# A selective state-space loop with its three elementwise steps dealt out anew: input product on the vector engine from PSUM, decay in PSUM, output product on GpSimd

## The chip, the cores and the metric

The kernel runs on one core of a Trainium2 chip. The metric is the device time in microseconds (us) of one execution. The kernel before was timed three times: 2757.33, 2756.4 and 2756.42 us, so the median is 2756.42 us.

A core has five engines with instruction queues of their own: TensorE (PE, matrix products), VectorE (DVE), ScalarE (ACT), GpSimd (POOL) and SyncE (SP, which here only starts DMAs). Each runs its own program in order. They are tied together by semaphores: an instruction adds to a semaphore when it has finished, and `wait_ge(s, n)` holds the queue of an engine until the semaphore `s` has reached `n`. SBUF is the on-chip memory of 128 partitions; PSUM is the smaller one that TensorE writes, here 8 banks of 128x512 f32 numbers.

## The reference, cut to what matters

The input is x of shape (4, 1024, 128), that is 4 batches of 1024 positions and 128 features. A layer has a state-space part (`_L0_attn_ref`) and an attention part with a mixture of 32 experts (`_L0_ffn_ref`). The change is in the state-space part alone, in these lines:

```python
Bm = h @ w_B.T + b_B                      # (batch, 1024, 16)
Cm = h @ w_C.T + b_C                      # (batch, 1024, 16)
Delta = softplus((h @ w_d1.T + b_d1) @ w_d2.T + b_d2)
A_bar = exp(-Delta[..., None] * A)        # decay, one for each of the 16 states
BX = (Delta * h)[..., None] * Bm[:, :, None, :]
# states[t] = A_bar[t] * states[t-1] + BX[t], along the 1024 positions
_, states = associative_scan(comb, (A_bar, BX), axis=1)
y = einsum('blfn,bln->blf', states, Cm) + D * h
```

For each batch and for each of 16 states four 128x1024 arrays are made (features on the partitions, positions along the row): the decay, the driving term bx = (Delta h) B, the state by a running scan, and the product cs = state x C. The 16 products are summed to y.

## The kernel before, in words

The batches are done one after the other (`Fori(0, BATCH)` on every engine). Each has a state-space stage, then eight head pairs of attention, then the experts. The stages are closed by `part_end`, which all five engines must reach. The order within a stage is written out by hand: each engine has its own instruction list, and only semaphores order one against another.

The state loop runs over n = 0 to 15. It uses PSUM bank pairs 2-3 (the row of B spread over all partitions), 4-5 (the row of C spread likewise) and 6-7 (the sum y). The steps of one state are:

- PE `broadcast_b` (line 1271): two bf16 products that write the B row of state n into banks 2-3. PE `broadcast_c` (line 1279): the same for C in banks 4-5.
- ACT line 712: copies banks 2-3 into `b_rows` in SBUF. ACT line 717: the decay, exp of `delta` times a column, into `decay` in SBUF.
- POOL line 538: bx = `du` x `b_rows`, all in SBUF.
- DVE line 964: the scan, `state` from `decay` and `bx`. DVE line 970: cs = `state` x banks 4-5.
- PE `add_state` (line 1286): adds cs into banks 6-7 by a product with the identity, two calls of 512 columns in f32; the trace has them as four matmul records.

`decay`, `b_rows`, `bx`, `state` and `cs` have two buffers each, which alternate with n. Semaphores for free buffers start above zero (`CREDITS`, line 365). So `cs_ready`, which starts at 2, reaches i + 3 when the product cs of state i is made, and `add_state(i)` waits for exactly that.

PE's list before is broadcast_b(0), b(1), c(0), and then for m = 0 to 13: broadcast_b(m+2), broadcast_c(m+1), add_state(m); at the end c(15), add(14), add(15). DVE's list is scan(n), product(n), for each n. After the loop DVE line 972 multiplies banks 6-7 with the gate, and what follows it is the output norm and projection of the stage. Before the loop DVE line 957 makes `du`; its signal is `delta_ready`.

Of the kernel before, what the change touches and what calls it, by code (L numbers as in the profile page):

```python
# [7 lines left out]
ALU = mybir.AluOpType  # L8
ACT = mybir.ActivationFunctionType
AX_X = mybir.AxisListType.X  # L10
F32 = mybir.dt.float32
# [3 lines left out]
P = 128  # L15
BATCH, SEQ, DM = 4, 1024, 128
# [4 lines left out]
STATES = 16  # L21
# [138 lines left out]
def program(nc, ins, out):  # L160
    with ExitStack() as ctx:
        def sb(name, shape, dt=F32, where=None):
            return (where or ctx).enter_context(nc.sbuf_tensor(name, shape, dt))

        def sem(name):
            return ctx.enter_context(nc.semaphore(name))
# [9 lines left out]
        neg_a = sb("neg_a", [P, STATES])  # L176
# [48 lines left out]
        m_ctx = ExitStack()  # L225
# [12 lines left out]
        sp_log = sb("sp_log", [P, SEQ], F32, m_ctx)  # L238
        delta = sb("delta", [P, SEQ], F32, m_ctx)
        du = sb("du", [P, SEQ], F32, m_ctx)  # L240
        decay = sb("decay", [P, 2, SEQ], F32, m_ctx)
        b_rows = sb("b_rows", [P, 2, SEQ], F32, m_ctx)
        bx = sb("bx", [P, 2, SEQ], F32, m_ctx)
        state = sb("state", [P, 2, SEQ], F32, m_ctx)
        cs = sb("cs", [P, 2, SEQ], F32, m_ctx)
# [66 lines left out]
        def banks(a, n=2):  # L312
            return ps[:, a:a + n, :].rearrange("p a n -> p (a n)")
# [5 lines left out]
        passed, part_done, weights_in = sem("passed"), sem("part_done"), sem("weights_in")  # L319
# [10 lines left out]
        a_out, a_taken = sem("a_out"), sem("a_taken")  # L330
        v_out, v_taken = sem("v_out"), sem("v_taken")
        tok_ready, v_norm, yg_ready = sem("tok_ready"), sem("v_norm"), sem("yg_ready")

        bc_out, bc_ready, delta_ready = sem("bc_out"), sem("bc_ready"), sem("delta_ready")
        b_bcast, b_taken, c_bcast = sem("b_bcast"), sem("b_taken"), sem("c_bcast")
        decay_ready, bx_ready, scanned, cs_ready, cs_used = (
            sem("decay_ready"), sem("bx_ready"), sem("scanned"), sem("cs_ready"), sem("cs_used"))

# [3 lines left out]
        proj_out, proj_taken = sem("proj_out"), sem("proj_taken")  # L342
# [16 lines left out]
        moe_taken, y_stored = sem("moe_taken"), sem("y_stored")  # L359
# [2 lines left out]


        DOWN_FREE = HALVES * SLOTS
        CREDITS = [(proj_out, 2 * 10), (y_stored, 16), (a_taken, 2), (v_taken, 2), (scanned, 2), (bx_ready, 2),
                   (cs_used, 2), (b_taken, 1), (cs_ready, 2),
                   (proj_taken, PROJ_BANKS), (scores_taken, 3), (blocks_taken, 2), (pv_out, NU), (v_added, ADDS), (p_added, ADDS),
                   (ctx_ready, 4),
                   (high_a, 1), (high_p, 1), (low_ready, 1), (roped_ready, 1), (inverted, 1), (misc_taken, 1),
# [21 lines left out]
        PARTS, V_ANGLES, V_FIRST, V_STEPS, V_OUTS, A_OUTS, A_STEPS = 3, 14, 23, 118, 6, 20, 7  # L391
# [20 lines left out]
        def root_at(b, k):  # L412
            return 2 + b * RSTDS + k + 1
# [75 lines left out]
        def _(pool):  # L489
            for s, c in CREDITS:  # L490
                pool.sem_inc(s, c)
# [18 lines left out]
            def inverse_root(at, n, eps=EPS):  # L510

                pool.wait_ge(ms_ready, at)
                pool.sem_inc(passed, 1)
                pool.tensor_scalar(ms[:, 0:n], ms[:, 0:n], eps, None, ALU.add).then_inc(ms_plus, 1)
                pool.wait_ge(ms_plus, at)
                pool.tensor_tensor(rstd[:, 0:n], ms[:, 0:n], neg_half[:, 0:n], ALU.pow).then_inc(rstd_ready, 1)
# [3 lines left out]
            with pool.Fori(0, BATCH) as b:  # L520
# [6 lines left out]
                                              b_out_r.unsqueeze(1).broadcast_to((P, TILES, P)), ALU.add))  # L527
                inverse_root(root_at(b, R_CONV), 1)

                pool.wait_ge(delta_ready, b + 1)  # L530
                pool.sem_inc(passed, 1)
                with pool.Fori(0, STATES // 2) as r:
                    for k in range(2):
                        n = b * STATES + 2 * r + k
                        pool.wait_ge(b_taken, n + 2)

                        pool.wait_ge(scanned, n + 1)
                        pool.tensor_tensor(bx[:, k, :], du[:, :], b_rows[:, k, :], ALU.mult).then_inc(bx_ready, 1)  # L538
                inverse_root(root_at(b, R_GATED), TILES)
                part_end(pool, PARTS * b + 2)  # L540

# [20 lines left out]
                def step(s, par, this, prev, prev2):  # L562
# [4 lines left out]
                    for k in range(2 if this else 0):  # L567
# [9 lines left out]
                        for i in (2 * k, 2 * k + 1):  # L577
                            pool.sem_inc(passed, 1)
                            pool_copy(pool, *copies[i]).then_inc(high_p, 1)
                            pool.wait_ge(high_p, 4 * n + i + 2)  # L580
                            pool.sem_inc(passed, 1)
                    for kind, _, u in slots(prev, this):
                        if kind == "low":

# [67 lines left out]
        def _(act):  # L652
# [20 lines left out]
            with act.Fori(0, BATCH) as b:  # L673
                def take(k, n, dst, func, bias=0.0, scale=1.0):

                    act.wait_ge(a_out, b * A_OUTS + k + 1)
                    act.activation(dst, ps[0:n, k % 2, :], func, bias=bias, scale=scale).then_inc(a_taken, 1)
# [25 lines left out]
                act.preload_act_table(ACT.Exp)  # L703
                for c in range(2):
                    take(10 + c, 96, bc3[:, c * HALF:(c + 1) * HALF], ACT.Identity)
                with act.Fori(0, STATES // 2) as r:
                    for k in range(2):
                        n = b * STATES + 2 * r + k
                        act.wait_ge(b_bcast, n + 1)

                        act.wait_ge(bx_ready, n + 1)
                        act.activation(b_rows[:, k, :], banks(2), ACT.Copy).then_inc(b_taken, 1)  # L712
                        act.wait_ge(delta_ready, b + 1)

                        act.wait_ge(scanned, n + 1)
                        act.sem_inc(passed, 1)
                        act.activation(decay[:, k, :], delta[:, :], ACT.Exp,
                                       scale=neg_a[:, bass.ds(2 * r + k, 1)]).then_inc(decay_ready, 1)
                for c in range(2):
                    take(12 + c, P, gT[:, c * HALF:(c + 1) * HALF], ACT.Identity)  # L720
                part_end(act, PARTS * b + 2)
# [111 lines left out]
        def _(dve):  # L833
# [93 lines left out]
            with dve.Fori(0, BATCH) as b:  # L927
# [27 lines left out]
                dve.wait_ge(a_step, A_STEPS * b + 6)  # L955
                st.link(dve.scalar_tensor_tensor(delta[:, :], z[:, :], 0.0, sp_log[:, :], ALU.max, ALU.add))
                dve.tensor_tensor(du[:, :], delta[:, :], h_act[:, :], ALU.mult).then_inc(delta_ready, 1)
                with dve.Fori(0, STATES // 2) as r:
                    for k in range(2):
                        n = b * STATES + 2 * r + k  # L960
                        dve.wait_ge(decay_ready, n + 1)
                        dve.wait_ge(bx_ready, n + 3)
                        dve.wait_ge(cs_ready, n + 1)
                        dve.tensor_tensor_scan(state[:, k, :], decay[:, k, :], bx[:, k, :], 0.0, ALU.mult, ALU.add  # L964
                                               ).then_inc(scanned, 1)
                        dve.wait_ge(scanned, n + 3)
                        dve.wait_ge(c_bcast, n + 1)

                        dve.wait_ge(cs_used, n + 1)
                        dve.tensor_tensor(cs[:, k, :], state[:, k, :], banks(4), ALU.mult).then_inc(cs_ready, 1)  # L970
                dve.wait_ge(cs_used, STATES * b + STATES + 2)
                dve.tensor_tensor(hc[:, :], banks(6), gate[:, :], ALU.mult).then_inc(yg_ready, 1)

# [223 lines left out]
        def _(pe):  # L1197
# [13 lines left out]
            def cut(t, c, shift=0):  # L1211
                return t[:, c * HALF + shift:(c + 1) * HALF + shift]
# [19 lines left out]
            with pe.Fori(0, BATCH) as b:  # L1232
# [33 lines left out]

                def broadcast_b(i):

                    pe.wait_ge(b_taken, b * STATES + i + 1)
                    for c in range(2):  # L1270
                        made = pe.matmul(ps[:, 2 + c, :], fold[:, bass.ds(i, 1)].broadcast_to((96, P)),
                                         cut(bc3, c), start=True, stop=True)
                    made.then_inc(b_bcast, 1)

                def broadcast_c(i):

                    pe.wait_ge(cs_ready, b * STATES + i + 2)
                    for c in range(2):
                        made = pe.matmul(ps[:, 4 + c, :], fold[:, bass.ds(STATES + i, 1)].broadcast_to((96, P)),
                                         cut(bc3, c), start=True, stop=True)  # L1280
                    made.then_inc(c_bcast, 1)

                def add_state(i, k):
                    pe.wait_ge(cs_ready, b * STATES + i + 3)
                    for c in range(2):
                        made = pe.matmul(ps[:, 6 + c, :], ident[:, :], cut(cs[:, k, :], c), start=False, stop=False,  # L1286
                                         skip_group_check=True)
                    made.then_inc(cs_used, 1)

                broadcast_b(0)  # L1290
                broadcast_b(1)
                broadcast_c(0)
                with pe.Fori(0, STATES // 2 - 1) as r:
                    for k in range(2):
                        broadcast_b(2 * r + k + 2)
                        broadcast_c(2 * r + k + 1)
                        add_state(2 * r + k, k)
                broadcast_c(STATES - 1)
                add_state(STATES - 2, 0)
                add_state(STATES - 1, 1)  # L1300
# [305 lines left out]
```

## Time and profile before

| What | Value |
|---|---|
| Median of three runs | 2756.42 us |
| Span of the profiled execution | 2757.4 us |
| PE busy (share of the span) | 2292.2 us (83%) |
| DVE busy | 2103.8 us (76%) |
| POOL busy | 1243.0 us (45%) |
| ACT busy | 1162.1 us (42%) |
| Scans, line 964, 64 of them | 207.4 us |
| bx on POOL, line 538, 64 | 171.4 us |

The profile is of one execution whose own time is its span, 2757.4 us, with nothing told beside it; that is 1.0 us above the median. Busy shares are means over stages with quite different limits. The profile also gives the TensorE clock that was granted in a stretch, as a share of the full 2.4 GHz: 1.00 is 2.4 GHz, 0.50 is 1.2 GHz, and a figure between them is a mean over a stretch with both. "Idle before, releaser" tells how long an engine stood idle ahead of an instruction and which other instruction ended that.

### The profile page before, as it was taken

What the parts mean: (1) busy time and instruction counts of PE and PEld (TensorE: products, weight loads), DVE (VectorE), ACT (ScalarE), POOL (GpSimd) and SP (SyncE); (2) the same over time, 40 slices, a digit from 0 to 9 for tenths busy, and PEclk for the clock granted to TensorE, in tenths of its full rate; (3) what the DMA queues carried; (4) which work ended last, traced back from release to release, by engine and by line L of the source; (5) the groups of instructions that cost most, each with busy time, mean ns of one, the idle gap of its engine ahead of it and who ended that gap; (6) DMA issues with size and microseconds to landing.
All of it is one profiled execution on the core that took longest, in us unless ns stands there. A gap on an engine that the chain in (4) does not pass through costs nothing.

```text
span 2757.4 us, 45423 instructions
## 1 busy us (share of the span) xinstructions
PE 2292.2 (83%) x11606; PEld 1361.5 (49%) x11606; DVE 2103.8 (76%) x3267; ACT 1162.1 (42%) x1889; POOL 1243.0 (45%) x1058
## 2 busy tenths in 40 slices
PE   3649999879665999997966599999796669999889
PEld 1235555547323555554732455564572245555456
DVE  4868888769496888876948688886794878888678
ACT  3413443337541434344743143443474223434256
POOL 2544555433253646443325465554333455556332
PEclk9779999989886999998978799999897879999889
DMA  1000000001000000000100000000100000000011
GB/s 56 0 23 5 5 8 4 0 19 41 11 0 23 5 9 4 4 0 25 36 9 0 23 5 9 4 4 1 31 30 9 0 23 5 8 8 0 3 34 33
DMA packets 36374, 35.84 MB, mean 13 GB/s; under 512 B 4008, under 2 KB 31120, under 8 KB 36240
## 3 DMA queue, kind: packets, MB, share of 16 engines
q1 hardware_dynamic: 36240, 34.27, 4.2%
q8 instruction: 58, 0.95, 0.1%
q14 instruction: 76, 0.62, 0.1%
HBM read 32.16 MB, written 2.10 MB: 12 GB/s over the span
## 4 chain that ended last, share of the span: by engine, by line
PE 58%; DVE 18%; issue 10%; ACT 7%; POOL 5%; DVEq 1%; ACTq 0%; DMA 0%; POOLq 0%; SPq 0%
PE ps L1431 8%; PE ps L1446 7%; PE ps L1216 6%; PE ps L1217 5%; PE ps L1218 5%; PE ps L1413 4%; DVE state L964 4%; PE ps L1415 3%; PE ps L1332 3%; PE ps L1286 3%; POOL bx L538 3%; PE ps L1491 2%; ACT q_split L750 2%; PE ps L1244 2%; DVE inverse L1007 2%
## 5 line engine op out<-in xcount | busy, mean ns | idle before, releaser
L767 ACT ACTIVATE probs<-ps 128x512 f32<-128x512 f32 (+3 forms) x768 | 356.5, 488 | 510.8 <-PE ps L1418 282.0
L1071 DVE TENSOR_REDUCE tops<-ps 128x1 f32<-128x512 f32 (+3 forms) x768 | 387.7, 545 | 116.7 <-PE ps L1446 81.7
L612 POOL TENSOR_TENSOR prob_sums<-prob_sums,probs 128x512 f32<-128x512 f32 (+3 forms) x256 | 237.8, 929 | 334.4 <-ACT probs L767 322.5
L1446 PE MATMUL ps<-k_high,q_split 128*128 128x512 f32 (+3 forms) x768 | 323.0, 435 | 41.9 <-POOL k_high L484 35.0
L1413 PE MATMUL ps<-q_split,k_high 128*128 128x512 f32 (+3 forms) x768 | 324.5, 423 | 21.8 <-ACT probs L767 15.5
L1431 PE MATMUL ps<-probs,vals 128*64 128x512 f32 (+3 forms) x1536 | 325.4, 509 | 0.0
L1415 PE MATMUL ps<-q_max,k_low 65*128 65x512 f32 (+7 forms) x768 | 268.9, 350 | 0.0
L1446 PEld LDWEIGHTS ps<-k_high,q_split 128*128 128x128 f32 x768 | 159.1, 208 | 218.0 <-issue 112.0
L574 POOL TENSOR_TENSOR roped<-turned 128x1024 f32<-128x1024 f32 x64 | 155.4, 2429 | 239.2 <-DVE turned L1048 226.3
L538 POOL TENSOR_TENSOR bx<-du,b_rows 128x1024 f32<-128x1024 f32 x64 | 171.4, 2691 | 199.9 <-ACT b_rows L712 163.8
L964 DVE TENSOR_TENSOR_SCAN state<-decay,bx 128x1024 f32<-128x1024 f32 x64 | 207.4, 3240 | 42.9 <-POOL bx L538 42.9
L742 ACT ACTIVATE q_max<-ps 1x512 fp32r<-1x512 f32 x128 | 75.2, 588 | 377.1 <-PE ps L1332 376.3
L1174 DVE TENSOR_TENSOR hg_low<-hg,hg_high 128x512 fp32r<-128x512 f32 x256 | 231.3, 903 | 0.7 <-ACT hg_high L805 0.7
L797 ACT ACTIVATE hid<-ps,cols 128x512 f32<-128x512 f32 x256 | 176.5, 689 | 101.9 <-PE ps L1218 73.8
L1413 PEld LDWEIGHTS ps<-q_split,k_high 128*128 128x128 f32 x768 | 151.3, 197 | 121.2 <-ACT probs L767 84.3
L1169 DVE TENSOR_TENSOR hg<-hid,ps 128x512 f32<-128x512 f32 x256 | 174.6, 682 | 46.9 <-ACT hid L797 35.2
L484 POOL TENSOR_SCALAR w_high<-w 128x256 fp32r<-128x256 f32 x128 | 56.6, 442 | 282.9 <-PE ps L1218 280.4
L1098 DVE TENSOR_TENSOR prob_sums<-prob_sums,probs 128x512 f32<-128x512 f32 (+3 forms) x256 | 181.1, 707 | 0.4
L805 ACT ACTIVATE hg_high<-hg 128x512 fp32r<-128x512 f32 x256 | 159.4, 623 | 1.9 <-PE ps L1218 1.4
L1286 PE MATMUL ps<-cs,ident 128*128 128x512 f32 x256 | 152.4, 730 | 0.0
L1216 PE MATMUL ps<-hg_high,w_high 128*128 128x512 f32 x256 | 149.5, 584 | 2.6 <-DVE hg_low L1174 2.6
L1415 PEld LDWEIGHTS ps<-q_max,k_low 65*128 65x128 f32 (+1 forms) x768 | 149.0, 194 | 4.1
(230 smaller groups left out, 4937.6 us busy)
## 6 DMA issues: line engine op xcount, KB each, us to landing
w<-in_w SPq DMA_DIRECT2D x128, 128.0 KB, 2.1
w_pair<-in_w_pairs SPq DMA_DIRECT2D x36, 256.0 KB, 2.6
xin<-in_x SPq DMA_DIRECT2D x5, 512.0 KB, 3.8
out<-acc SPq DMA_DIRECT2D x4, 512.0 KB, 4.1
pos<-in_c_pos SPq DMA_DIRECT2D x1, 512.0 KB, 4.8
v_w<-in_v_w SPq DMA_DIRECT2D x1, 512.0 KB
o_w<-in_o_w SPq DMA_DIRECT2D x1, 512.0 KB
v_b<-in_v_b SPq DMA_DIRECT2D x1, 512.0 KB
```

Of the source, the lines that this page charges most:

```text
L538: pool.tensor_tensor(bx[:, k, :], du[:, :], b_rows[:, k, :], ALU.mult).then_inc(bx_ready, 1)
L612: pool.tensor_tensor(total, before, probs[:, u % RING, 1, at:HALF], ALU.add).then_inc(p_added, 1)
L767: act.activation(probs[:, u % RING, h, q0 - HALF * c:HALF], ps[:, 4 + h, 0:w], ACT.Exp, scale=SCALE).then_inc(blocks_taken, 1)
L964: dve.tensor_tensor_scan(state[:, k, :], decay[:, k, :], bx[:, k, :], 0.0, ALU.mult, ALU.add).then_inc(scanned, 1)
L1071: dve.tensor_reduce(tops[:, h, u:u + 1], ps[:, MX_BANK[u % 3], 0:w], AX_X, ALU.max).then_inc(scores_taken, 1)
L1174: dve.tensor_tensor(hg_low[:, buf, :], hg[:, buf, :], hg_high[:, buf, :].bitcast(F32), ALU.subtract).then_inc(hg_low_ready, 1)
L1216: pe.matmul(o, w_high, x_high, start=first, stop=False, skip_group_check=True)
L1286: made = pe.matmul(ps[:, 6 + c, :], ident[:, :], cut(cs[:, k, :], c), start=False, stop=False, skip_group_check=True)
L1413: pe.matmul(o, k_high[1 - par][h][:, j * P:(j + 1) * P], q_split[1 - par][h][:, q0:q0 + w], start=True, stop=False)
L1415: made = pe.matmul(o, k_low[1 - par][h][rows_k, j * P:(j + 1) * P], q_max[1 - par][h][rows_k, q0:q0 + w], start=False, stop=not own)
L1431: made = pe.matmul(ps[HD * g:HD * (g + 1), CTX_BANK[c], at:HALF], vals[1 - par][:, j, g, :], probs[:, u % RING, g, at:HALF], start=(j == 0 ...
L1446: made = pe.matmul(o, q_split[par][h][:, i * P:(i + 1) * P], k_high[par][h][:, k0:k0 + w], start=True, stop=not own)
```

## The change

The three elementwise steps around the scan get other engines and other places:

- bx = `du` x B is now made by DVE straight from PSUM banks 2-3. ACT's copy of the B row and the tensor `b_rows` are gone.
- The decay is written by ACT to PSUM banks 0-1, one buffer, and the scan reads it there. The tensor `decay` is gone.
- cs = `state` x C is now made by POOL. It reads C from a new SBUF tensor `c_rows` (two buffers), to which ACT copies banks 4-5.
- DVE's list is drive(0), then drive(n+1), scan(n) for n = 0 to 13, then drive(15), scan(14), scan(15).
- PE's list is b(0), c(0), then for m = 0 to 13: b(m+1), c(m+1), add(m), then b(15), c(15), add(14), add(15). Banks 2-3 are free by `bx_ready` (DVE's product), banks 4-5 by `c_taken` (ACT's copy).

The core of the diff:

```diff
@@ CREDITS
-(scanned, 2), (bx_ready, 2), (cs_used, 2), (b_taken, 1), (cs_ready, 2),
+(scanned, 2), (bx_ready, 1), (cs_used, 2), (c_taken, 1), (cs_ready, 2),
@@ POOL
-                        pool.wait_ge(b_taken, n + 2)
-                        pool.wait_ge(scanned, n + 1)
-                        pool.tensor_tensor(bx[:, k, :], du[:, :], b_rows[:, k, :], ALU.mult).then_inc(bx_ready, 1)
+                        pool.wait_ge(c_taken, n + 2)
+                        pool.wait_ge(scanned, n + 3)
+                        pool.wait_ge(cs_used, n + 1)
+                        pool.tensor_tensor(cs[:, k, :], state[:, k, :], c_rows[:, k, :], ALU.mult).then_inc(cs_ready, 1)
@@ ACT
-                        act.wait_ge(b_bcast, n + 1)
-                        act.wait_ge(bx_ready, n + 1)
-                        act.activation(b_rows[:, k, :], banks(2), ACT.Copy).then_inc(b_taken, 1)
-                        act.wait_ge(delta_ready, b + 1)
-                        act.wait_ge(scanned, n + 1)
-                        act.sem_inc(passed, 1)
-                        act.activation(decay[:, k, :], delta[:, :], ACT.Exp,
+                        act.wait_ge(scanned, n + 2)
+                        act.activation(banks(0), delta[:, :], ACT.Exp,
                                        scale=neg_a[:, bass.ds(2 * r + k, 1)]).then_inc(decay_ready, 1)
+                        act.wait_ge(c_bcast, n + 1)
+                        act.wait_ge(cs_ready, n + 1)
+                        act.activation(c_rows[:, k, :], banks(4), ACT.Copy).then_inc(c_taken, 1)
@@ DVE
-                with dve.Fori(0, STATES // 2) as r:
+                dve.wait_ge(delta_ready, b + 1)
+                def drive(n, k):
+                    dve.wait_ge(b_bcast, n + 1)
+                    dve.wait_ge(scanned, n + 1)
+                    dve.tensor_tensor(bx[:, k, :], du[:, :], banks(2), ALU.mult).then_inc(bx_ready, 1)
+                def scan(n, k):
+                    dve.wait_ge(bx_ready, n + 2)
+                    dve.wait_ge(decay_ready, n + 1)
+                    dve.wait_ge(cs_ready, n + 1)
+                    dve.tensor_tensor_scan(state[:, k, :], banks(0), bx[:, k, :], 0.0, ALU.mult, ALU.add
+                                           ).then_inc(scanned, 1)
+                drive(b * STATES, 0)
+                with dve.Fori(0, STATES // 2 - 1) as r:
                     for k in range(2):
                         n = b * STATES + 2 * r + k
-                        dve.wait_ge(decay_ready, n + 1)
-                        dve.wait_ge(bx_ready, n + 3)
-                        dve.wait_ge(cs_ready, n + 1)
-                        dve.tensor_tensor_scan(state[:, k, :], decay[:, k, :], bx[:, k, :], 0.0, ALU.mult, ALU.add
-                                               ).then_inc(scanned, 1)
-                        dve.wait_ge(scanned, n + 3)
-                        dve.wait_ge(c_bcast, n + 1)
-                        dve.wait_ge(cs_used, n + 1)
-                        dve.tensor_tensor(cs[:, k, :], state[:, k, :], banks(4), ALU.mult).then_inc(cs_ready, 1)
+                        drive(n + 1, 1 - k)
+                        scan(n, k)
+                drive(b * STATES + STATES - 1, 1)
+                scan(b * STATES + STATES - 2, 0)
+                scan(b * STATES + STATES - 1, 1)
@@ PE
                 def broadcast_b(i):
-                    pe.wait_ge(b_taken, b * STATES + i + 1)
+                    pe.wait_ge(bx_ready, b * STATES + i + 1)
                 def broadcast_c(i):
-                    pe.wait_ge(cs_ready, b * STATES + i + 2)
+                    pe.wait_ge(c_taken, b * STATES + i + 1)
                 broadcast_b(0)
-                broadcast_b(1)
                 broadcast_c(0)
                 with pe.Fori(0, STATES // 2 - 1) as r:
                     for k in range(2):
-                        broadcast_b(2 * r + k + 2)
+                        broadcast_b(2 * r + k + 1)
                         broadcast_c(2 * r + k + 1)
                         add_state(2 * r + k, k)
+                broadcast_b(STATES - 1)
                 broadcast_c(STATES - 1)
                 add_state(STATES - 2, 0)
                 add_state(STATES - 1, 1)
```

## Rows read from the trace of the kernel before

**Rows 1.** The page's head and its first part: busy time, share, instructions.

```profile
span 2757.4 us, 45423 instructions
PE 2292.2 (83%) x11606; PEld 1361.5 (49%) x11606; DVE 2103.8 (76%) x3267; ACT 1162.1 (42%) x1889; POOL 1243.0 (45%) x1058
```

**Rows 2.** Busy time and clock in the four loop stretches: the first, their sum.

```profile
69.80:156.70 86.90, 58.29 (x133) 21.63 (x131) 71.91 (x34) 34.58 (x34) 42.69 (x16) 0.78 0.00 0
...
sum 345.60, PE 230.17 PEld 85.50 DVE 287.48 ACT 138.24 POOL 171.39; mean PE 57.54 PEld 21.37 DVE 71.87 ACT 34.56 POOL 42.85
```

**Rows 3.** Durations by line (ns: least, median, most) of the loop's elementwise steps.

```profile
L964 DVE TENSOR_TENSOR_SCAN state<-decay,bx x64: 2283/3407/4430, 76.2 to 2187.5; 128x1024 f32<-128x1024 f32 x64
...
L970 DVE TENSOR_TENSOR cs<-state,ps x64: 1220/1221/1222, 80.7 to 2189.8; 128x1024 f32<-128x1024 f32 x64
...
L538 POOL TENSOR_TENSOR bx<-du,b_rows x64: 2334/2353/4238, 73.9 to 2181.8; 128x1024 f32<-128x1024 f32 x64
...
L717 ACT ACTIVATE decay<-delta,neg_a x64: 1138/1139/1150, 73.6 to 2181.3; 128x1024 f32<-128x1024 f32 x64
```

**Rows 4.** Timeline, entry of the first loop: start, duration, engine, operation, idle before.

```profile
69.80 1.23 DVE L957 TENSOR_TENSOR du<-delta,h_act 128x1024 f32<-128x1024 f32 x1
...
73.86 4.64 POOL L538 TENSOR_TENSOR bx<-du,b_rows 128x1024 f32<-128x1024 f32 x2 [20.79 <-ACT b_rows L712]
...
76.23 4.42 DVE L964 TENSOR_TENSOR_SCAN state<-decay,bx 128x1024 f32<-128x1024 f32 x1 [5.21 <-POOL bx L538]
```

**Rows 5.** Timeline, first states of the first loop, low clock.

```profile
77.05 1.02 ACT L712 ACTIVATE b_rows<-ps 128x1024 f32<-128x1024 f32 x1 [0.16 <-PE ps L1271]
...
80.72 2.35 POOL L538 TENSOR_TENSOR bx<-du,b_rows 128x1024 f32<-128x1024 f32 x1 [2.23 <-DVE state L964]
...
82.44 0.76 PEld L1286 LDWEIGHTS ps<-cs,ident 128*128 128x128 f32 x2 [0.28 <-issue]
82.87 3.62 PE L1286 MATMUL ps<-cs,ident 128*128 128x512 f32 x4
...
86.28 1.06 PE L1271 MATMUL ps<-bc,fold 96*128 96x512 bf16 x2
...
87.38 1.02 ACT L712 ACTIVATE b_rows<-ps 128x1024 f32<-128x1024 f32 x1 [5.40 <-PE ps L1271]
```

**Rows 6.** Timeline, the same loop a state on, full clock.

```profile
88.72 1.22 DVE L970 TENSOR_TENSOR cs<-state,ps 128x1024 f32<-128x1024 f32 x1
...
90.08 0.11 PEld L1279 LDWEIGHTS ps<-bc,fold 96*128 x2 [0.58 <-issue]
...
90.31 0.41 PEld L1286 LDWEIGHTS ps<-cs,ident 128*128 128x128 f32 x2
90.52 1.88 PE L1286 MATMUL ps<-cs,ident 128*128 128x512 f32 x4
...
92.24 0.60 PE L1271 MATMUL ps<-bc,fold 96*128 96x512 bf16 x2
```

**Rows 7.** Timeline of PE after a gap of idle time, and the end of the loop.

```profile
115.82 1.03 PE L1279 MATMUL ps<-bc,fold 96*128 96x512 bf16 x2 [3.86 <-DVE cs L970]
116.65 3.62 PE L1286 MATMUL ps<-cs,ident 128*128 128x512 f32 x4
120.06 1.06 PE L1271 MATMUL ps<-bc,fold 96*128 96x512 bf16 x2
...
150.47 6.16 PE L1286 MATMUL ps<-cs,ident 128*128 128x512 f32 x8
...
156.67 1.23 DVE L972 TENSOR_TENSOR hc<-ps,gate 128x1024 f32<-128x1024 f32 x1 [3.62 <-PE ps L1286]
```

**Rows 8.** Busy time in stretches of the first loop (order PE, PEld, DVE, ACT, POOL), clock.

```profile
84.00:88.00 4.00, 4.00 (x8) 1.39 (x8) 3.96 (x3) 0.62 (x1) 0.00 (x0) 0.58 0.00 0
...
112.00:116.00 4.00, 0.18 (x1) 0.13 (x2) 3.97 (x3) 2.17 (x2) 1.70 (x2) 0.83 0.00 0
...
120.00:124.00 4.00, 4.00 (x12) 1.55 (x11) 3.74 (x3) 2.08 (x3) 1.67 (x1) 0.81 0.00 0
```

More of the change, by code:

```diff
@@ L240, in program @@
         du = sb("du", [P, SEQ], F32, m_ctx)
-        decay = sb("decay", [P, 2, SEQ], F32, m_ctx)
-        b_rows = sb("b_rows", [P, 2, SEQ], F32, m_ctx)
+        c_rows = sb("c_rows", [P, 2, SEQ], F32, m_ctx)
         bx = sb("bx", [P, 2, SEQ], F32, m_ctx)
@@ L334, in program @@
         bc_out, bc_ready, delta_ready = sem("bc_out"), sem("bc_ready"), sem("delta_ready")
-        b_bcast, b_taken, c_bcast = sem("b_bcast"), sem("b_taken"), sem("c_bcast")
+        b_bcast, c_bcast, c_taken = sem("b_bcast"), sem("c_bcast"), sem("c_taken")
         decay_ready, bx_ready, scanned, cs_ready, cs_used = (
@@ L364, in program @@
         DOWN_FREE = HALVES * SLOTS
-        CREDITS = [(proj_out, 2 * 10), (y_stored, 16), (a_taken, 2), (v_taken, 2), (scanned, 2), (bx_ready, 2),
-                   (cs_used, 2), (b_taken, 1), (cs_ready, 2),
+        CREDITS = [(proj_out, 2 * 10), (y_stored, 16), (a_taken, 2), (v_taken, 2), (scanned, 2), (bx_ready, 1),
+                   (cs_used, 2), (c_taken, 1), (cs_ready, 2),
                    (proj_taken, PROJ_BANKS), (scores_taken, 3), (blocks_taken, 2), (pv_out, NU), (v_added, ADDS), (p_added, ADDS),
@@ L528, in _ @@
                 inverse_root(root_at(b, R_CONV), 1)
-                pool.wait_ge(delta_ready, b + 1)
                 pool.sem_inc(passed, 1)
@@ L705, in _ @@
                     take(10 + c, 96, bc3[:, c * HALF:(c + 1) * HALF], ACT.Identity)
+                act.wait_ge(delta_ready, b + 1)
+                act.wait_ge(a_taken, b * A_OUTS + 12 + 2)
+                act.sem_inc(passed, 1)
                 with act.Fori(0, STATES // 2) as r:
```

## The prediction

> **What bounds the kernel now.** I read the page's head first, to see that no engine is busy all the time [rows 1]: 83% for PE is a mean over stages, and the changed loop is one stage of a batch. The stretches of that loop come next [rows 2]: from the start of DVE's `du` to the start of line 972 it takes 86.9 us in the first batch and 345.6 us in all four, an eighth of the span. In it DVE is busy 287.5 of 345.6 us, POOL half, PE two thirds at a mean clock of 0.78. So the loop runs at some 5 us a state and DVE and POOL set it together. The durations show how [rows 3]: the scan takes 2.28 us at least and 4.43 at most, bx on POOL 2.35 and up to 4.24, while the product with PSUM on DVE is 1.22 each time. A long scan is a short one plus a bx (2.28 + 2.15): whichever of the two starts second waits for the other. One state costs about 2.28 + 2.35 us, and the 1.22 of line 970 lies beside POOL's work.
>
> Last I read the timeline for the order of the queues. ACT's copy of the second B row ended at 77.05 + 1.02 = 78.07 us, and with that banks 2-3 were free. Yet PE made the next B row only at 86.28, after the four records of `add_state` at 82.87, and ACT waited 5.40 us for it [rows 5]. PE's list is strictly in order: a B row that stands behind an `add_state` waits for it, whether its bank is free or not. Before, this does little harm, since the B row two states ahead is made ahead of `add_state(m)`.
>
> **The change, part by part.**
>
> Off DVE goes line 970 (1.22 us a state), and a product of the same kind and size comes on, one operand from PSUM: 1.22 us [rows 3]. No change in DVE's sum. Off POOL goes bx, and cs comes on, the same shape with both operands in SBUF: I take the 2.35 us of bx; ends are DVE's 1.22 for such a product and the stretched 4.24. ACT has a copy of 1.02 us [rows 5] and an exp of 1.14 [rows 3] as before; for the exp into PSUM I take 1.14, between the copy's 1.02 and twice that. The scan with its decay in PSUM isn't in the trace: below I set the 1.22 of a DVE pass with a PSUM operand, above the 4.43 of a scan that waits, and take 2.28, the same operation unhindered.
>
> The price lies in what stands behind what. After the change PE's list is b(m+1), c(m+1), add(m), b(m+2). DVE's list is drive(m+2), scan(m+1). Drive(m+2) needs the B row m+2, that row stands behind add(m) on PE, add(m) waits for POOL's cs(m), and cs(m) waits for scan(m). So scan(m+1) cannot start until the whole output path of state m has been walked. It is a ring with one state in flight:
>
> - scan 2.28 [rows 3];
> - to POOL 0.07, from the scan that ends at 80.65 to the bx at 80.72 [rows 4, 5];
> - cs on POOL 2.35;
> - to PE 0.14, from the end of line 970 at 89.94 to the load at 90.08 [rows 6];
> - `add_state` and the B row at full clock: load to product 90.31 to 90.52, 0.21; product to B row 90.52 to 92.24, 1.72; B row 0.60 [rows 6]. At half clock 0.43, 3.41 and 1.06 [rows 5];
> - to the reader 0.04, from 87.34 to 87.38 [rows 5];
> - drive on DVE 1.22, and 0.03 to the next instruction.
>
> At full clock a state takes 8.66 us, at half clock 11.03 us. DVE works 3.50 us of it.
>
> Which clock? PE will work about 3 us a state at full clock or 5.7 at half, and stand idle for 5.3 to 5.7 us. Today, after the last PE work ahead of 112, the stretch from 112 to 116 has 0.83, so the clock fell to half in it, before work came back at 115.82, and that work ran at half clock: 1.03, 3.62 and 1.06 us [rows 7, 8]. Full clock came back in the stretches 84 to 88 (mean 0.58, so near 87.4, 5.4 us after the work began at about 82) and 120 to 124 (0.81, near 121.5, 5.7 us after) [rows 8]. A gap in the ring is longer than this one, so most bursts begin at half clock and some get full clock before they end. I take 10.4 us a state, three quarters of the way from 8.66 to 11.03.
>
> The Trainium skill bears on it ("TensorE: Matmul & The Clock Gate", section on HAM oscillation): where PE waits between bursts for long enough, each burst starts at half clock again. By that rule every state has the 11.03 us; the rows above show the fall and the cold burst, and whether each burst stays cold to its end they don't show. That is the third case below.
>
> Now a batch. Entry: bx began at 73.86 after a copy of 1.02 and 0.17 of signal, so the first B row is there at 72.67. Then drive(0) 1.22, the second B row some 1.2, drive(1) 1.22, and scan(0) starts near 76.4, against 76.23 now; from 69.80 that is 6.6 us [rows 4]. Then 14 turns of the ring, since scan(n) for n = 1 to 14 waits for drive(n+1). Scan(14) takes 2.28. Scan(15) has its drive made already and follows after the decay (0.17 + 1.14); cs(15) is done 6.1 us after scan(14) ended. The tail: cs(14) 2.42 with its signal, 0.57 to the first product, then eight records of `add_state` in a row, 6.16 now [rows 7]: 9.2 us. Sum: 6.6 + 14 x 10.4 + 2.28 + 9.2 = 163.7 us, four times 654.8 us. In place of 345.6 us [rows 2] that is 309 us more. From the profile's own 2757.4 us I come to 3067 us, and to 3066 us against the median of the runs, which is 1 us lower.
>
> What is hidden: ACT's exp and copy (2.2 us) start when a scan ends and have the 6.4 to 8.7 us until the next scan; without that cover the exp would stand between two scans at 1.14 + 0.2 us. The wait for `delta_ready` that now stands ahead of ACT's loop holds one exp of 1.14 us, which DVE's first two drives cover. POOL's products and DVE's scans no longer overlap save at scan(15), where at most 1 us a batch is lost. DMAs are not moved; SP does nothing in the loop, and behind `part_end` all comes later as a block.
>
> **The rivals.**
>
> *The same ring at full clock.* For it: PE was granted 0.78 on average in the loop [rows 2]. Against it: the fall at a shorter gap [rows 8]. 6.6 + 14 x 8.66 + 11.5 = 139.3, four times 557, so 2969 us. 10 in 100.
>
> *The same ring, every burst at half clock to the end.* For it: the cold records after the gap [rows 7]. Against it: full clock came back 5.4 and 5.7 us after the start of work [rows 8], which is about a burst's length. 6.6 + 14 x 11.03 + 11.5 = 172.5, four times 690, so 3102 us. 17 in 100.
>
> *The other side: the ring does not close, and DVE sets the pace.* If a B row is ready whenever DVE comes to a drive, a state is scan 2.28, then the exp of 1.14 with its 0.2 of signals, beside which the drive of 1.22 lies: 3.62 us. POOL's 2.42 fits in it, and what is gained is that the scan no longer waits for POOL's products. 6.6 + 15 x 3.62 + 2.28 + 4.6 for cs and add at full clock = 67.8, four times 271, so 2683 us, 2.7% faster. It decides from the point at which B row m+2 is ready before scan(m) ends. For it: DVE has only 3.5 us a state. Against it: the 86.28 of a B row whose bank was free since 78.07 [rows 5]. Should the scan still exclude POOL's product there, a state is 2.28 + 2.35 + 0.1 and the time 2748 us, 0.3% faster: the change would not do what it says. The two together 7 in 100. On that point the Trainium skill ("SBUF — State Buffer", section on the two separate sides) says that a DVE operation with two SBUF inputs locks the port pair which GpSimd needs, each for its whole instruction. The 2.28 to 4.43 us of the scan and the even 1.22 of line 970 agree; by it the scan with its decay in PSUM is free, and the 2683 us would hold in this case.
>
> *The ring with another scan.* If the scan from PSUM costs 1.22 or 4.43, the time moves by 64 x (-1.06) = -68 or 64 x 2.15 = +138 us. A cs on POOL of 1.22 or 4.24 would give -72 or +121 us. Little speaks for either, as each has a row of its own kind. 4 in 100.
>
> **How the numbers follow.** The forecast, the ring at 10.4 us a state, has 62 in 100 and gives 3066 us. The range takes in the full clock (2969) and half clock (3102) with some 15 us on each side for signals and the tail: 2955 to 3117 us. That leaves out the faster rival and most of the last, about 1 in 10. Two kernels can be told apart at about 0.2%, 5.5 us. All cases of the ring are slower by far more: slower 0.92, faster 0.07, same 0.01.
>
> **What would show it.** In the trace after, the starts of two scans of one batch should lie 8.7 to 11 us apart for n = 1 to 14, and scan(15) about 3.6 us behind scan(14). Each scan should take 2.28 us and each POOL product 2.35, with no long ones among them. DVE should idle some 5 to 7 us ahead of each drive, released by PE's B row (line 1271's successor), PE some 5.5 us ahead of each `add_state`, released by POOL's product, and POOL ahead of each product by the scan. The mean clock in the loop should fall below 0.78, toward 0.6, and DVE's busy time in it to near 4 x 57 us ([rows 2], with scans of 2.28 us in place of a mean near 3.24, the 207.4 us of line 964 over 64). Attention and experts should keep their times to within a few us. I am wrong in the main thing if drives follow scans without a wait for PE; wrong in size if the add and the B row together take far from 4 to 5 us.

## The result and the profile after

The changed kernel takes 3064.19 us (median of four, 3061.38 to 3065.93). The kernel before, run beside it, takes 2756.88 us. The ratio is 1.1111 with a 95% interval of 1.1095 to 1.1127: 11% slower, as forecast, and 2 us from the forecast of 3066 us.

The head of the page after, first part, answers to [rows 1]:

```profile
span 3061.8 us, 45303 instructions
PE 2375.4 (78%) x11606; PEld 1385.4 (45%) x11606; DVE 2042.3 (67%) x3267; ACT 1161.1 (38%) x1889; POOL 1222.4 (40%) x1058
```

DVE and POOL do less work than before in a longer span. PE is busy 83 us more, at a mean clock of 0.858 against 0.901, and still only 78% of the span. So no engine became a bound by its own work. Next the costliest groups of the loop on the same page. The columns are busy time and mean ns of one, then the idle time just ahead of them with what ended it:

```profile
L1298 PE MATMUL ps<-cs,ident 128*128 128x512 f32 x256 | 233.6, 1069 | 327.7 <-POOL cs L537 327.7
...
L537 POOL TENSOR_TENSOR cs<-state,c_rows 128x1024 f32<-128x1024 f32 x64 | 150.0, 2343 | 552.3 <-DVE state L971 552.3
...
L964 DVE TENSOR_TENSOR bx<-du,ps 128x1024 f32<-128x1024 f32 x64 | 78.2, 1221 | 396.9 <-PE ps L1283 396.9
```

Read the last column as a circle: PE's `add_state` waits for POOL's product, POOL's product for DVE's scan, and DVE's drive, which stands ahead of the next scan, for PE's B row (line 1283). Each waits 5 to 9 us a state for the one before.

One turn of it in the timeline, first loop (start, duration, engine, operation, idle before):

```profile
84.39 2.28 DVE L971 TENSOR_TENSOR_SCAN state<-ps,bx 128x1024 f32<-128x1024 f32 x1
86.76 2.35 POOL L537 TENSOR_TENSOR cs<-state,c_rows 128x1024 f32<-128x1024 f32 x1 [8.22 <-DVE state L971]
...
89.16 3.78 PE L1298 MATMUL ps<-cs,ident 128*128 128x512 f32 x4 [5.08 <-POOL cs L537]
...
92.73 1.06 PE L1283 MATMUL ps<-bc,fold 96*128 96x512 bf16 x2
...
93.83 1.22 DVE L964 TENSOR_TENSOR bx<-du,ps 128x1024 f32<-128x1024 f32 x1 [7.15 <-PE ps L1283]
94.97 2.28 DVE L971 TENSOR_TENSOR_SCAN state<-ps,bx 128x1024 f32<-128x1024 f32 x1
```

The B row, which has nothing to do with cs, starts 3.57 us after `add_state` has begun, and the drive follows at its end. From scan to scan it is 10.58 us here. Later in the loop the clock comes back during the burst, so that the B row takes 0.72 us instead of 1.06 and the spacing falls to 10.2 or 10.3:

```profile
173.09 3.78 PE L1298 MATMUL ps<-cs,ident 128*128 128x512 f32 x4 [5.50 <-POOL cs L537]
176.66 0.72 PE L1283 MATMUL ps<-bc,fold 96*128 96x512 bf16 x2
```

The stretch of the first loop (busy PE, PEld, DVE, ACT, POOL, then the clock), for the first of [rows 2]:

```profile
67.30:230.00 162.70, 80.13 (x133) 27.28 (x131) 56.04 (x33) 34.20 (x34) 37.49 (x16) 0.63 0.00 0
```

It took 86.9 us before and takes 162.7 now. The four loops take 162.7, 159.8, 162.8 and 159.5 us, together 644.8 in place of 345.6: 299 of the 304 us by which the span grew. The durations of the two steps (ns: least, median, most) show that nothing is slow in itself:

```profile
L971 DVE TENSOR_TENSOR_SCAN state<-ps,bx x64: 2281/2283/2291, 73.7 to 2489.6; 128x1024 f32<-128x1024 f32 x64
L537 POOL TENSOR_TENSOR cs<-state,c_rows x64: 2341/2343/2347, 76.2 to 2492.0; 128x1024 f32<-128x1024 f32 x64
```

The long scans of [rows 3] are gone. These durations alone don't show that the scan no longer waits for POOL: in this kernel a POOL product lies beside a scan only at scan(15), once a batch. e5 shows it below. And 11% are lost all the same, to the order of two lists, as e1, e3 and e5 show.

### The profile page after: what moved, and what is told of

It reads as the page before. It is cut to its first block and busy times, and to the rows that moved or that the text cites. A ratio compares the mean times of both kernels' runs of the same rounds, so it can differ in the third digit from the quotient of the medians.

```text
span 3061.8 us, 45303 instructions
## 1 busy us (share of the span) xinstructions
PE 2375.4 (78%) x11606; PEld 1385.4 (45%) x11606; DVE 2042.3 (67%) x3267; ACT 1161.1 (38%) x1889; POOL 1222.4 (40%) x1058
## 5 line engine op out<-in xcount | busy, mean ns | idle before, releaser
L1298 PE MATMUL ps<-cs,ident 128*128 128x512 f32 x256 | 233.6, 1069 | 327.7 <-POOL cs L537 327.7
L537 POOL TENSOR_TENSOR cs<-state,c_rows 128x1024 f32<-128x1024 f32 x64 | 150.0, 2343 | 552.3 <-DVE state L971 552.3
L964 DVE TENSOR_TENSOR bx<-du,ps 128x1024 f32<-128x1024 f32 x64 | 78.2, 1221 | 396.9 <-PE ps L1283 396.9
L1298 PEld LDWEIGHTS ps<-cs,ident 128*128 128x128 f32 x256 | 73.6, 317 | 431.5 <-POOL cs L537 367.6
L712 ACT ACTIVATE ps<-delta,neg_a 128x1024 f32<-128x1024 f32 x64 | 71.5, 1118 | 480.5 <-DVE state L971 478.5
```

## The experiments

**e1: the B row ahead of `add_state`.**

```diff
@@ PE, in the changed kernel
                 broadcast_b(0)
+                broadcast_b(1)
                 broadcast_c(0)
...
-                        broadcast_b(2 * r + k + 1)
+                        broadcast_b(2 * r + k + 2)
                         broadcast_c(2 * r + k + 1)
                         add_state(2 * r + k, k)
-                broadcast_b(STATES - 1)
```

> The changed kernel with one edit: TensorE makes B row m+2 ahead of add_state(m), as the kernel before did, not B row m+1. Theory (the ring through the B row behind add_state costs the time): the ring opens, scans stand 3.6 us apart (scan 2.28, decay 1.14, signals 0.2), a batch's loop takes about 68 us from du to the gate product, and the whole 2683 us. Rival (the scan still excludes GpSimd's product though its decay is in PSUM): scans of up to 4.6 us, 4.7 us apart, 2748 us. Rival (the loss has another cause, such as the single decay buffer or GpSimd itself): scans stay 9 us or more apart, near 3064 us.

2765.94 us, ratio to before 1.0028 (1.0018 to 1.0037). Nearly all of the loss is gone, and my number was still wrong by 83 us. DVE's scans, with one of the drives between them, tell why:

```profile
92.63 2.28 DVE L971 TENSOR_TENSOR_SCAN state<-ps,bx 128x1024 f32<-128x1024 f32 x1
...
96.27 2.29 DVE L971 TENSOR_TENSOR_SCAN state<-ps,bx 128x1024 f32<-128x1024 f32 x1
...
101.58 1.22 DVE L964 TENSOR_TENSOR bx<-du,ps 128x1024 f32<-128x1024 f32 x1 [3.03 <-PE ps L1283]
102.72 2.28 DVE L971 TENSOR_TENSOR_SCAN state<-ps,bx 128x1024 f32<-128x1024 f32 x1
...
106.35 2.29 DVE L971 TENSOR_TENSOR_SCAN state<-ps,bx 128x1024 f32<-128x1024 f32 x1
...
112.65 2.28 DVE L971 TENSOR_TENSOR_SCAN state<-ps,bx 128x1024 f32<-128x1024 f32 x1
```

The spacings alternate, 3.6 and 6.4 us: two states share 10 us. The ring is not open, it is one state longer. B row m+3 now stands behind `add_state(m)`, and its drive stands ahead of scan(m+2), so scan(m) reaches scan(m+2). The drive at 101.58 is such a one: its B row came 3 us after the scan of 96.27 had ended. I had counted only that the row for scan(m+1) was free.

**e3: the drive behind the scan.** The same ring cut at another place.

```diff
@@ DVE, in the changed kernel
-                        drive(n + 1, 1 - k)
                         scan(n, k)
+                        drive(n + 1, 1 - k)
...
-                drive(b * STATES + STATES - 1, 1)
                 scan(b * STATES + STATES - 2, 0)
+                drive(b * STATES + STATES - 1, 1)
                 scan(b * STATES + STATES - 1, 1)
```

> The changed kernel with VectorE's list turned: scan(n), drive(n+1) in place of drive(n+1), scan(n); TensorE's list stays as changed. Theory (the ring is closed by the drive that stands ahead of the scan): scan(m) then reaches scan(m+2) instead of scan(m+1) through the same ring, so a state costs half of it, 4.3 us at full clock to 5.5 at half, about 4.8; time 2740 to 2812 us, about 2767. Rival (only TensorE's list matters, and every B row behind add_state costs the full ring): scans stay some 10 us apart, near 3060 us.

2758.56 us, ratio 1.0005 (0.9996 to 1.0015), within the range and 8 us below the middle. The rival is out: TensorE's list is as in the slow kernel and the loss is gone. Here too the scans come in pairs:

```profile
111.47 2.29 DVE L971 TENSOR_TENSOR_SCAN state<-ps,bx 128x1024 f32<-128x1024 f32 x1 [0.19 <-DVE bx L964]
115.11 2.29 DVE L971 TENSOR_TENSOR_SCAN state<-ps,bx 128x1024 f32<-128x1024 f32 x1 [0.24 <-DVE bx L964]
121.76 2.29 DVE L971 TENSOR_TENSOR_SCAN state<-ps,bx 128x1024 f32<-128x1024 f32 x1 [0.19 <-DVE bx L964]
```

**e5: both edits.**

> The edits of e1 and e3 together: B row m+2 ahead of add_state(m), and scan(n) ahead of drive(n+1). After e1 and e3 the theory is: each edit alone lengthened the ring's reach from one state to two (two states share 8.4 us at full clock to 10.5 at half), and together they make it three. Then 8.4/3 = 2.8 to 10.5/3 = 3.5 us a state is less than the 3.6 us of scan, drive and signals, the ring no longer binds, TensorE is busy 3 of 3.6 us and keeps full clock; about 68 us a batch's loop, 2685 us, at most 2710. Rival (what remains in e1 and e3 is TensorE's own work at half clock, 5.7 us a state, and not the ring's reach): scans stay near 5 us apart, 2740 us or more.

2685.39 us, ratio 0.9739 (0.9723 to 0.9755): 2.6% faster than the kernel before. The number was met within a microsecond. Its first loop, and two states of it:

```profile
69.60:136.60 67.00, 52.80 (x133) 17.40 (x131) 55.90 (x34) 35.14 (x34) 37.64 (x16) 0.90 0.00 0
```

```profile
97.23 2.29 DVE L971 TENSOR_TENSOR_SCAN state<-ps,bx 128x1024 f32<-128x1024 f32 x1 [0.19 <-ACT ps L712]
...
99.44 1.20 DVE L964 TENSOR_TENSOR bx<-du,ps 128x1024 f32<-128x1024 f32 x1
99.66 1.12 ACT L712 ACTIVATE ps<-delta,neg_a 128x1024 f32<-128x1024 f32 x1 [0.39 <-DVE state L971]
99.68 2.35 POOL L537 TENSOR_TENSOR cs<-state,c_rows 128x1024 f32<-128x1024 f32 x1 [1.32 <-DVE state L971]
...
100.87 2.29 DVE L971 TENSOR_TENSOR_SCAN state<-ps,bx 128x1024 f32<-128x1024 f32 x1 [0.23 <-DVE bx L964]
```

Scans are 3.6 us apart; drive, decay and POOL's product all lie beside one another. DVE is busy 55.9 of 67.0 us and stands still only some 0.2 us ahead of each scan. ScalarE's exp is just as close a bound: it starts when a scan has ended and ends at 100.78 us, after the drive (100.64) and just ahead of the next scan (100.87). Of the 64 scans 34 are released by the drive and 30 by the exp, so the two chains are level, and no run separates them.

The durations of all 64 scans, most of which have a POOL product beside them, as the one at 100.87 has:

```profile
L971 DVE TENSOR_TENSOR_SCAN state<-ps,bx x64: 2290/2291/2292, 73.9 to 2110.8; 128x1024 f32<-128x1024 f32 x64
```

**e2 and e7: the changed kernel with TensorE kept at work in its gap.**

```diff
@@ PE, in the changed kernel; idle_rhs holds zeros; FILL = 16 in e2, 24 in e7
                         broadcast_c(2 * r + k + 1)
+                        for f in range(FILL):
+                            pe.matmul(ps[:, 6 + f % 2, :], identb[:, :], idle_rhs[:, :], start=False, stop=False, ...)
                         add_state(2 * r + k, k)
```

> The changed kernel, its order kept, with 16 products of 512 columns with zeros added into the y banks between C row m+1 and add_state(m), so that TensorE works through most of its gap; the sum is unchanged. Theory (a state is a ring of 8.66 us at full clock, and the 1.75 us above that are TensorE's half clock): the granted clock in the loop rises above 0.95, scans stand 8.7 us apart, a time near 2970 us. Rival (the spacing of 10.4 us is latency that the clock has no part in): 10.4 us stay, near 3064 us or more, as the added products can only be in the way.

3014.21 us, ratio 1.0932 (1.0913 to 1.0950). The gain is about half of what was expected, and the first loop's clock is 0.86, not above 0.95. PE's rows of that loop:

```profile
129.47 3.62 PE L1312 MATMUL ps<-idle_rhs,identb 128*128 128x512 bf16 x16
135.21 3.68 PE L1301 MATMUL ps<-cs,ident 128*128 128x512 f32 x4 [2.13 <-POOL cs L540]
138.68 0.64 PE L1286 MATMUL ps<-bc,fold 96*128 96x512 bf16 x2
```

The added products run at full clock, 2.1 us stay idle, and the `add_state` behind them is at half clock (3.68, where 1.98 is seen in other states). States come in two main kinds, 8.4 and 10.0 us apart, with a few between.

> As e2_filled with 24 products in place of 16, so that at full clock 5.1 us of the 5.6 us gap are filled. In e2 states came in two kinds, 8.4 us and 10.0 us apart, the second where the clock fell in the 2 us that stayed idle. Theory: without that rest the clock stays full after each loop's start, nearly all states are 8.4 us, the loop's clock is above 0.95, 2950 to 2985 us. Rival (8.4 and 10 have another cause): both kinds remain in like number, near 3014 us.

2963.46 us, ratio 1.0745 (1.0727 to 1.0763). After a first spacing of 9.2 us, all states of the first loop but the last, which is outside the ring, are 8.4 us apart, and its clock is 0.95:

```profile
100.02 2.28 DVE L974 TENSOR_TENSOR_SCAN state<-ps,bx 128x1024 f32<-128x1024 f32 x1
108.39 2.28 DVE L974 TENSOR_TENSOR_SCAN state<-ps,bx 128x1024 f32<-128x1024 f32 x1
```

So of the 307 us lost, 101 are TensorE's half clock in the ring (3064 less 2963, if the added products did nothing else), and the rest is its length at full clock.

**e8: C back on VectorE, the ring kept.** GpSimd's product and ScalarE's C copy go; behind the scan DVE makes cs from PSUM.

```diff
@@ DVE, in scan(n, k)
+                    dve.wait_ge(scanned, n + 3)
+                    dve.wait_ge(c_bcast, n + 1)
+                    dve.wait_ge(cs_used, n + 1)
+                    dve.tensor_tensor(cs[:, k, :], state[:, k, :], banks(4), ALU.mult).then_inc(cs_ready, 1)
@@ PE, broadcast_c(i)
-                    pe.wait_ge(c_taken, b * STATES + i + 1)
+                    pe.wait_ge(cs_ready, b * STATES + i + 2)
```

> The changed kernel, its orders kept, with the product with C back on VectorE from PSUM (its 1.22 us right behind the scan), without the C copy on ScalarE and without GpSimd's product. Theory (the ring runs through GpSimd's 2.35 us): each state is shorter by 2.42 - 1.25 = 1.2 us, so about 9.2 us, the ring still closed; 64 x 1.2 = 75 us less, near 2987 us. Rival (moving C to GpSimd was itself the loss, not the place of the B row): the time falls back to near 2760 us.

3044.19 us, ratio 1.1039 (1.1020 to 1.1057): 20 us less than the changed kernel, not 75. The rival, that GpSimd's product was the loss, is out. The rows show where the 1.2 us went:

```profile
113.16 2.28 DVE L958 TENSOR_TENSOR_SCAN state<-ps,bx 128x1024 f32<-128x1024 f32 x1
115.48 1.22 DVE L963 TENSOR_TENSOR cs<-state,ps 128x1024 f32<-128x1024 f32 x1
...
116.84 1.03 PE L1282 MATMUL ps<-bc,fold 96*128 96x512 bf16 x2 [4.86 <-DVE cs L963]
117.67 3.62 PE L1289 MATMUL ps<-cs,ident 128*128 128x512 f32 x4
121.08 1.06 PE L1274 MATMUL ps<-bc,fold 96*128 96x512 bf16 x2
122.18 1.22 DVE L951 TENSOR_TENSOR bx<-du,ps 128x1024 f32<-128x1024 f32 x1 [5.48 <-PE ps L1274]
```

The C row shares its banks with DVE's product, so it now has to wait for it and stands in the ring ahead of `add_state`, 0.83 us; and the burst is at half clock to its end. A state is 10.16 us. My edit took one thing off the ring and put another on, which I had not counted.

**e4 and e6: the decay back in SBUF, two buffers;** e4 on top of e1, e6 on top of e5.

```diff
-                        act.wait_ge(scanned, n + 2)
-                        act.activation(banks(0), delta[:, :], ACT.Exp,
+                        act.wait_ge(scanned, n + 1)
+                        act.activation(decay[:, k, :], delta[:, :], ACT.Exp,
...
-                    dve.tensor_tensor_scan(state[:, k, :], banks(0), bx[:, k, :], 0.0, ALU.mult, ALU.add
+                    dve.tensor_tensor_scan(state[:, k, :], decay[:, k, :], bx[:, k, :], 0.0, ALU.mult, ALU.add
```

> As e1_b_row_ahead, but the decay goes back to SBUF with two buffers, so the scan reads two SBUF operands. Theory (a scan with two SBUF operands and GpSimd's product exclude each other, and the decay in PSUM frees them): 2.28 + 2.35 + 0.1 = 4.7 us a state, some scans of 4.4 us, about 2749 us, slower than e1 by some 65 us. Rival (nothing excludes, the long scans before had another cause): VectorE alone bounds at 3.55 us, since the decay is off the path, about 2676 us, no slower than e1.

2769.27 us, ratio 1.0042 (1.0027 to 1.0056). Inconclusive for the time: the scans are longer (median 3.08 us, up to 3.43), but e1's ring of two states had the room to hide it.

> As e5_both_orders, with the decay back in SBUF in two buffers. Theory (with the ring open the mutual exclusion of a scan with two SBUF operands and GpSimd's product decides): a state costs 2.28 + 2.35 + 0.1 = 4.7 us, or more if products are held up, scans up to 4.5 us, 2745 to 2765 us. Rival (the decay in PSUM bought nothing): within 0.3% of e5.

2743.91 us, ratio 0.9944 (0.9928 to 0.9961), 59 us slower than e5 and 1 us below my range. With the ring open it shows in the time. DVE's scans, and one product of POOL:

```profile
96.45 3.51 DVE L972 TENSOR_TENSOR_SCAN state<-decay,bx 128x1024 f32<-128x1024 f32 x1
100.03 2.34 POOL L538 TENSOR_TENSOR cs<-state,c_rows 128x1024 f32<-128x1024 f32 x1 [2.23 <-DVE state L972]
...
101.26 3.27 DVE L972 TENSOR_TENSOR_SCAN state<-decay,bx 128x1024 f32<-128x1024 f32 x1 [0.19 <-DVE bx L965]
105.67 3.50 DVE L972 TENSOR_TENSOR_SCAN state<-decay,bx 128x1024 f32<-128x1024 f32 x1
```

These scans are 1.0 to 1.2 us longer than 2.29, about the part of POOL's product that is still running when the scan starts (until 102.37 us at the scan of 101.26), and a state is 4.6 us on average. The first scan of each loop, which has no product beside it, takes 2.29 us with the same decay in SBUF, so it is not the place of the operand alone.

**e9: `add_state` one state later still.** PE's loop is b(m+2), c(m+1), add(m-1), with DVE's list as in e5.

> As e5_both_orders, with add_state one state later in TensorE's list: b(m+2), c(m+1), add(m-1). The ring then reaches four states on. Theory (in e5 the scan, the decay and the drive set 3.6 us a state, the ring only costs in the first states of a loop at half clock, one spacing of 5.0 there): only those first spacings shrink, 1 to 1.5 us a batch, 2679 to 2686 us. Rival (the ring still binds e5 throughout): 3.5 us a state or less, under 2677 us.

2687.77 us, ratio 0.9752 (0.9735 to 0.9768), no different from e5's, and 2 us above my range. One early spacing shrank from 5.0 to 4.0 us in the first loop, which the whole doesn't show; all later ones are 3.6 us as in e5. So after its first states the ring no longer binds e5.

**e10: e5 with C back on VectorE,** with e8's edit.

> As e5_both_orders, with the product with C back on VectorE from PSUM, and no C copy and no product on GpSimd. Theory (with the ring open the engine that does the work decides, so moving C to GpSimd is a gain): VectorE has 2.29 + 1.22 + 1.22 = 4.73 us and signals, 4.8 us a state, near 2756 us, slower than e5 by about 70 us. Rival (the gain of e5 comes from the B product and the PSUM decay alone): within 10 us of e5.

2744.28 us, ratio 0.9954 (0.9937 to 0.9971), 59 us slower than e5, 12 below my number. DVE has no pause left but 0.2 us:

```profile
93.39 2.29 DVE L958 TENSOR_TENSOR_SCAN state<-ps,bx 128x1024 f32<-128x1024 f32 x1
95.71 1.22 DVE L963 TENSOR_TENSOR cs<-state,ps 128x1024 f32<-128x1024 f32 x1
96.85 1.21 DVE L951 TENSOR_TENSOR bx<-du,ps 128x1024 f32<-128x1024 f32 x1
98.25 2.29 DVE L958 TENSOR_TENSOR_SCAN state<-ps,bx 128x1024 f32<-128x1024 f32 x1 [0.19 <-DVE bx L951]
```

Two operations of 1.22 us stand in each state where e5 has one. So moving C to GpSimd is a gain of 59 us, once the lists allow it.

## Why the prediction was right, point by point

- *The ring.* Shown twice: by the waits of the changed kernel, which go round PE, POOL, DVE and PE, and by e1, e3 and e5. Each of two edits, on two different engines and changing no operation, takes 300 us away, and both together 379 us. That fits a closed circle of waits and no single slow step. The row that gave it away before was the B row at 86.28 whose bank was free since 78.07 [rows 5].
- *Its length.* I had 8.66 us at full and 11.03 at half clock. Measured: 8.4 (e7) and at most 10.65 (first states of the changed kernel). Three terms were priced too high. The product on DVE starts its scan 1.13 to 1.14 us after itself, not 1.25. From POOL to PE it is 0.05 us, not 0.14, and from the start of PE's burst to the B row it is 3.57 us, not 0.43 + 3.41.
- *The clock in it.* I took three quarters of the way to half clock, 10.4 us. The first loop has (219.54 - 73.75) / 14 = 10.41 us, the second (973.88 - 830.66) / 14 = 10.23. Since both ends were some 0.3 us too high, the true place between them is nearer to half clock, 0.8 to 0.9 of the way. The two errors cancel; 10.4 was partly luck. The granted clock, 0.63, is what "toward 0.6" said. The rule in the Trainium skill ("TensorE: Matmul & The Clock Gate", HAM oscillation) that such bursts start at half clock each time holds here: `add_state` took 3.78 us in the rows shown. That a burst then stays at half clock to its end, as I read the rule when I put every state at 11.03 us, the page does not say, and the B row of 0.72 us shows that it need not.
- *Entry and tail.* 163.7 us a batch was forecast, 162.7 and 159.8 came for the first two. In the first the entry took 6.4 us for 6.6, and from the start of scan(14) to the end of the stretch it was 10.5 us for 11.5. The sum, 309 us, was 299 in the loops. Another 5 us came elsewhere: the stretch ahead of the first loop is 2.5 us shorter, and three of the four behind a loop are 2.4 to 2.6 us longer. The cause of that stays open. Without it the median would lie some 7 us below the forecast, not 2: a part of the closeness is luck here too.
- *The scan from PSUM* costs 2.28 us, as its row before. It does not wait for POOL: in e5, where products run beside the scans, it is 2.290 to 2.292 us in 64 cases, and e6 in the same order has 3.3 to 3.6 in all but the first of each loop. The Trainium skill's rule of the locked port pair ("SBUF — State Buffer", the two separate sides) agrees with both.
- *The rival on the other side.* 2683 us was named for an open ring, and e5 measures 2685. The condition that I gave it, B row m+2 ready before scan(m) ends, was for DVE's list as changed. With that list no run meets it: e1 misses it in every second state, where the row comes 3 us after that end, and gets 2766. My error was in e1's expectation, which took that one edit to be enough. The ring has to reach three states, since two of them share some 10 us and three states of 3.6 us are more than that.

## What to carry to other kernels

Before moving an operation to another engine, write down for each queue what stands in front of what, and follow one result round until it comes back to where it started; the length of that circle divided by the number of iterations it spans is a floor on the time of one, whatever the engines' shares say. A product that a later stage needs should be issued ahead of an instruction that waits for an earlier stage. An edit that lengthens a circle from one iteration to two only halves it: compute whether two is enough, and find the slack by moving the order, which adds no operation.

## What of the hardware was not expected

In e2, after 3.62 us of products at full clock and only 2.1 us of idling, `add_state` ran at half clock for most or all of its time in more than half of the states (up to 3.68 us against 1.98; 34 of the 56 spacings in the ring are over 9 us). At the gaps before the change the fall had come in idle stretches of some 3.9 us [rows 7, 8], and I had thought 2 us safe. Rests of some 0.4 us ahead of `add_state`, in e7, kept 0.95. The length of the last rest alone does not tell, though. In e6 the rests ahead of the B row and of `add_state` were 1.35 and 0.28 us, and `add_state` still took 3.33 us:

```profile
105.77 0.60 PE L1284 MATMUL ps<-bc,fold 96*128 96x512 bf16 x2 [1.35 <-DVE bx L965]
...
107.08 3.33 PE L1299 MATMUL ps<-cs,ident 128*128 128x512 f32 x4 [0.28 <-POOL cs L538]
```
